# Pads between the tiles: every family of wide fp32r matmuls reads its two operands at another distance modulo 256 bytes

## What is computed

```python
x = x + attn(einsum('bct,bcd->bdt', x, style_w[style]), w_qkv, q_ln, k_ln, w_out)
y = einsum('bsi,boi->bso', x, adapter_w[adapter])
logits = y @ gate_w;  weights = top_k(logits, 2).values
h = relu(y @ up_w) ** 2
shared = h @ down_w
routed = ((y @ fc1_w) @ expert_w * weights.sum(-1)) @ fc2_w
x = x + layernorm(shared + routed) * gamma + beta
```

## Time and the profile before

| | before |
|---|---|
| median of two runs | 1131.38 us |
| the profiled execution's own time | 1133.51 us |
| its span, first to last instruction | 1131.7 us |
| granted TensorE clock, mean | 0.993 of full |
| TensorE matmuls busy | 1095.0 us, 97% |
| TensorE weight loads busy | 891.5 us, 79% |
| GpSimd busy | 714.3 us, 63% |
| VectorE busy | 675.8 us, 60% |
| ScalarE busy | 602.3 us, 53% |
| share of TensorE in the chain that ended last | 95% |

### The profile page before, as it was taken

How to read it: one execution, slowest core, us unless ns; L and a number is a source line. 1 busy time by engine, 2 the same in 40 slices (tenths; PEclk the granted TensorE clock), 3 DMA queues, 4 the chain that set the end, 5 groups by cost and what they waited for, 6 DMA issues and landing times.

```text
span 1131.7 us, 27403 instructions
## 1 busy us (share of the span) xinstructions
PE 1095.0 (97%) x10996; PEld 891.5 (79%) x10996; DVE 675.8 (60%) x1040; ACT 602.3 (53%) x985; POOL 714.3 (63%) x612
## 2 busy tenths in 40 slices
PE   5999999999999999999999999999999999999994
PEld 3877888888888888888877778787878888787883
DVE  5567667666667666766666245565655565554432
ACT  3466767677777677777776425334161625233220
POOL 4565878787878787878676463556455463533332
PEclk9999999999999999999999999999999999999997
DMA  7125464646454646566567953233414123030100
GB/s 275 40 78 167 157 209 159 211 154 212 159 207 158 215 154 213 177 213 157 200 216 253 368 162 90 84 98 104 110 47 135 56 89 98 29 84 28 47 28 37
DMA packets 95292, 160.77 MB, mean 142 GB/s; under 512 B 46400, under 2 KB 47168, under 8 KB 89792
## 3 DMA queue, kind: packets, MB, share of 16 engines
q1 hardware_dynamic: 79456, 118.16, 32.6%
q0 software_dynamic: 12224, 34.10, 9.4%
q10 hardware_dynamic: 3488, 6.78, 1.7%
HBM read 93.97 MB, written 42.47 MB: 121 GB/s over the span
## 4 chain that ended last, share of the span: by engine, by line
PE 95%; DMA 1%; issue 1%; DVE 1%; POOL 0%; ACT 0%; SPq 0%; DVEq 0%; ACTq 0%; POOLq 0%
PE bank L645 24%; PE pair L829 16%; PE bank L805 15%; PE bank L735 10%; PE bank L685 8%; PE bank L822 8%; PE pair L662 3%; PE bank L693 3%; PE pair L707 2%; PE bank L635 2%; PE bank L720 1%; PE bank L775 1%; PE bank L673 1%; DMA xt<-in_x,tile_rows 1%; PE bank L756 0%
## 5 line engine op out<-in xcount | busy, mean ns | idle before, releaser
L1672 POOL TENSOR_TENSOR w_lo<-w2t,w_hi 128x2048 fp32r<-128x2048 f32 x38 | 175.0, 4605 | 35.6 <-ACT w_hi L991 35.5
L645 PE MATMUL bank<-wqkv_hi,h_hi 128*128 128x512 f32 x384 | 154.5, 402 | 0.1
L645 PE MATMUL bank<-wqkv_hi,h_lo 128*128 128x512 f32 x384 | 150.5, 392 | 0.0
L645 PE MATMUL bank<-wqkv_lo,h_hi 128*128 128x512 f32 x384 | 150.3, 391 | 0.0
L1742 POOL TENSOR_TENSOR u_lo<-act,u_hi 128x512 fp32r<-128x512 f32 x64 | 82.8, 1294 | 103.3 <-ACT u_hi L1184 103.2
L829 PE MATMUL pair<-down_hi,u_hi 128*128 128x512 f32 x256 | 101.0, 394 | 0.0
L829 PE MATMUL pair<-down_hi,u_lo 128*128 128x512 f32 x256 | 100.8, 394 | 0.0
L805 PE MATMUL bank<-yT_hi,up_hi 128*128 128x512 f32 x256 | 100.8, 394 | 0.0
L829 PE MATMUL pair<-down_lo,u_hi 128*128 128x512 f32 x256 | 100.3, 392 | 0.0
L805 PE MATMUL bank<-yT_hi,up_lo 128*128 128x512 f32 x256 | 99.8, 390 | 0.0
L1521 DVE TENSOR_TENSOR act<-act 128x512 f32<-128x512 f32 x59 | 67.0, 1136 | 54.6 <-ACT act L1180 54.6
(11 more groups left out here) (178 smaller groups left out, 2910.7 us busy)
## 6 DMA issues: line engine op xcount, KB each, us to landing
w2t<-in_w SPq DMA_DIRECT2D x38, 1024.0 KB
vx<-v_hl SPq DMA_DIRECT2D x128, 68.0 KB
x1g<-x_rows SPq DMA_DIRECT2D x32, 256.0 KB, 3.0
kx<-k_hl SPq DMA_DIRECT2D x124, 64.0 KB
x_rows<-x1t SPq DMA_DIRECT2D x31, 256.0 KB, 3.5
ffn_high<-w_high SPq DMA_DIRECT2D x20, 256.0 KB, 3.5
ffn_low<-w_low SPq DMA_DIRECT2D x20, 256.0 KB, 3.4
stage<-in_wqkv SPq DMA_DIRECT2D x3, 1024.0 KB, 8.1
```

The source lines that it names most:

```text
L645: m = e.matmul(into, a[:, c, :], b[:, n, c, :], start=(c == 0 and k == 0), stop=(c == KC - 1 and k == 2))
L1672: e.tensor_tensor(w2_lo[:, :, :], w2t[:, :, :], w2_hi[:, :, :].bitcast(F32), ALU.subtract).then_inc(d_wlo, 1)
```

## The change

Nothing is computed otherwise and no instruction is added, removed or moved on any engine. Pads are put between tiles, the order of the four `h` tiles is changed, and the four chunks of `gate_hl` are put 256 bytes apart. All tiles behind the first of these edits shift by 768 to 1184 bytes.

```diff
-    gate_hl = sb("gate_hl", [P, KC, 2, EXPERTS], F32R)
+    gate_lines = sb("gate_hl", [P, KC, 64], F32R)
+    gate_hl = gate_lines[:, :, 0:2 * EXPERTS].rearrange("p c (a n) -> p c a n", a=2)
...
     w2_hi = sb("w2_hi", [P, KC, DM], F32R)
+    sb("pad_x", [P, 48])
     xgT_hi = sb("xgT_hi", [P, DM], F32R)
...
-    h_hi = [asb(f"h_hi{i}", [P, KC, P], F32R) for i in range(2)]
-    h_lo = [asb(f"h_lo{i}", [P, KC, P], F32R) for i in range(2)]
+    h_hi, h_lo = [], []
+    for i in range(2):
+        asb(f"pad_h{i}", [P, 8 + 8 * i])
+        h_hi.append(asb(f"h_hi{i}", [P, KC, P], F32R))
+        h_lo.append(asb(f"h_lo{i}", [P, KC, P], F32R))
...
+    asb("pad_kx", [P, 32])
     prep = ExitStack()
...
+    asb("pad_o", [P, 8])
     o_hi = asb("o_hi", [P, BPT, P], F32R)
...
     yt = sb("yt", [P, KC, 2, TOK], U16)
+    sb("pad_y", [P, 24])
     yT_hi = [sb("yT_hi0", [P, KC, TOK], F32R)]
...
-    sb("pad", [P, 160])
+    sb("pad", [P, 192])
     down_hi = sb("down_hi", [P, FC, DM], F32R)
```

## The result

The changed kernel takes **1143.0 us** (median of two runs, 1142.75 to 1143.25) against 1131.38 before. The recorded ratio is 1.0089, with a 95% interval of 1.0067 to 1.011: slower by about 1%, inside the 2% band. The two medians alone give 1.0103, from two runs on each side; why the recorded ratio is lower is not shown. The forecast was 1144.0.

What follows compares the result with a forecast made beforehand. TensorE was taken as the bound, its wide fp32r matmul pace passing into the time one for one. Terms 6.6 - 0.6 + 2.1 + 5.1 - 0.6 = +12.6 us on 1131.38 made 1144.0 us, range 1123 to 1156.

Steps and rivals of the forecast that it cites:

- project: Attention tiles, distance 0 to 32 and 96: 35 steps a tile slower by 6.7 ns, less entry and early waits; +6.0 us.
- adapt_slot: Distance 0 to 192: 10 steps slower by 6.7 ns, less entry, in 38 slots; +2.1 us.
- up: Feed-forward part, distance 0 to 160: 768 steps slower by 6.7 ns; +5.1 us.
- `down`, f = 4: Feed-forward chunk going from distance 128 to 0: 3 x 32 steps faster by 6.7 ns; -0.6 us.
- `out_project`, `down` f = 0 to 3: Distances 64 to 224 and 128 to 160: 233.3 ns before and after; 0, bounds -5.1 to +2.6 us each.
- route products, gates: Feed-forward route products stay at distance 0 and 226.7 ns; gate products go from mixed distances to 224; 0.
- at 226.7 from f = 5 on: Expected sign in the later profile: down x24 falls from 5.56 to 5.54 us, with this step in its later chunks.
- five others at 226.7: Argument that distance matters: two slow families sit at 233, the other families share nothing but their distance.
- Distance is not the cause: Rival: the tiles of down or neighbours of out_project make them slow; nothing moves, 1131.4 us; chance 0.12.
- The starts matter too: Rival: moving operands starting at odd multiples of 32 bytes cost 16 cycles themselves; 1149 us, range 1145 to 1157; chance 0.10.
- Cheap: Rival: new distances step at 220 ns, giving 1103 us, or only one or two do, 1115 to 1130; chance 0.15.
- dearer: Rival: new distances cost two collisions of 16 cycles, 240 ns a step; +34 us, 1165; chance 0.13 for 1152 to 1165.

Runs made afterwards that it cites:

- only_project: Kernel before the change, with project's operands moved to distances 32 and 96 and the other changed families kept at equivalent distances; ratio 1.0058 (1.0046 to 1.0071).
- only_up: Kernel before the change, with up moved to distance 160, down f = 0 to 3 to 32 and gates to 160; ratio 1.0052 (1.0034 to 1.0069).
- all_zero: Kernel before the change, with pads putting every wide matmul family and the gate products at distance 0; median 1126.8 us, ratio 0.9951.
- shift32: Kernel before the change, with one 32-byte pad ahead of gate_raw moving every later tile, all distances kept; ratio 0.9998 (0.9986 to 1.001).

## Why the prediction was right

**The bound.** TensorE's chain passed the slower pace on one for one: from the eighth attention tile to the last its gaps are at most 0.14 us, before and after; where the two parts of the kernel meet, its longest wait is 1.5 us before and 1.4 after. From the start of the ninth tile's `project` to that of the thirty-first, before took 18.88 us a tile and after 19.13: +0.25, where the terms say 0.26. From the first `up` to the last `down`, 511.1 and 516.7 us: +5.6.

**The size for distances that no row showed.** 233.3 ns was taken from 64 and 128 for 32, 96, 160, 192 and 224. Four of five fit within 1 ns; 192 did not. The quantum of 16 cycles is real as a mean at 32, 64, 128, 160 and 224 (558 to 560 cycles), but not as a rule: 192 stands at 549, 96 at 562.

| term | forecast us | measured us, from the pieces |
|---|---|---|
| `project` | +6.0 | +0.20 and +0.22 a tile, less the early tiles: +6.1 (only_project: +6.6) |
| `adapt_slot` | +2.1 | +0.02 in 26 slots, +0.02 to +0.04 in the others: about +0.9 (an estimate; a piece is read to 0.01) |
| `up` | +5.1 | 8 x 0.65 = +5.2 (only_up: +5.9) |
| `down`, f = 4 | -0.6 | 5.56 before and after: 0 |
| `out_project`, `down` f = 0 to 3 | 0 | 0 |
| route products, gates | 0 | 24 x 0.01 - 8 x 0.03 = 0 |
| sum | +12.6 | +12.2; medians +11.6; by the ratio +10.1 (7.6 to 12.4) |

**Two terms were mis-sized, and offset each other in part.** `adapt_slot` was priced at 233.3 and measured 230, because 192 is a cheap distance; 1.3 us too much. For f = 4 I counted three steps at 226.7, but the pace does not follow the distance at once. The distance fell to 0 at the 13th matmul in place of the 16th, and yet the steps from the 13th to the 21st take 1.85 us in both kernels and only the last three are at 226.7: the three matmuls that were won went into a longer settling, eight steps in place of five (974.88 - 973.73 = 1.15 us, 230 ns each, in the earlier trace rows). That is 0.6 us too much gain, and "at 226.7 from f = 5 on" was wrong for the same reason.

**A reading that was off.** The prediction set "five others at 226.7" against two slow families. There are four (`project`, `adapt_slot`, `up`, route products) and the end of `down`; `gate_products` stood at 233.8, and all_zero shows that the distance does not change that.

**The rivals.** "Distance is not the cause" fell with all_zero and shift32: the step of a matmul of 512 columns is 16 cycles longer or not through nothing but the distance between its two kinds of operands. The Trainium skill, "SBUF — State Buffer", section "Who interferes with whom", gives TensorE two independent read ports and says that it never waits on anyone. The runs here do not agree, for these shapes: `down` x24 went from 5.56 to 5.44 us by a move of its tiles. Whether the ports themselves or something behind them is where it waits, no run shows. "The starts matter too" fell with shift32. "Cheap" got one of its five distances, "dearer" none. The size was no more than well placed between them: that 32, 96, 160 and 224 would stand near 64 and 128 was taken over from two samples, and 192, 240 and 248 show that it need not have held.

**The start-up.** The second tile's `project` begins at 34.30 us before and at 31.64 after, in the chains. This isn't the change: shift32, which steps like before, has 31.80, all_zero 34.17. Two things make up the 2.7 us. The gathered x that TensorE's first `style` waits for came later: that `style` begins at 25.17 us before and at 23.99 after, 1.2 us. And TensorE's granted clock: from 27 to 29 us it is 0.50 before (the 1.2 GHz level) and 1.00 after. In front of the drop TensorE had waited 3.0 us for that x, after the change 2.0. So the x24 of the first `project` took 7.08 us before and 5.60 after, 1.5 us. all_zero has the same low stretch (0.50 from 26 to 28 us, behind a wait of 2.8), shift32 has none (1.00, a wait of 2.1): in these four traces the low clock goes with the longer wait, not with the pads. This start-up is why the two spans are nearer than the medians.

## What to carry to other kernels

Where TensorE is the bound and wide fp32r matmuls follow each other with a new stationary operand each, put the moving and the stationary tiles at the same address modulo 256 bytes. It costs a pad of under 256 bytes and was worth 3% of each such matmul, 0.5% of this kernel; a shift of all starts by 32 bytes was free. To find it, compare the step from start to start between families of one shape: a difference of a few nanoseconds with everything else equal is a finding. And when a family gets to distance 0 from another distance, or from behind small matmuls, do not count on the cheap pace at once. The settling took from none to ten steps in the `project` tiles of the kernel before, five steps in its `down`, eight in `down` after, at some 230 to 232 ns, and none in `down` of only_up; what sets its length stays open.

## What the runs showed that I had not expected

- The curve is no window: 240 (16 bytes behind) at 227.7 ns and 192 at 228.9 are nearly as cheap as 0, while 248, between 240 and 0, is at 233.3. Which resource has that pattern stays open.
- The cost is in the step of the matmuls alone; the weight loads of the wide families with 128 columns last 187 to 189 ns at every distance of the runs.
- At a fixed dear distance the steps are not alike: they alternate between 238 and 229 ns at 128 in `down` and between 236 and 231 at 64 in `out_project`, and go round in threes (232, 238, 231) at 160 in `down`, with means within a nanosecond of each other.
- With 16 stationary columns distance 0 brings nothing: 8 gate products took 1.86 us at 0 and 1.84 at 224.
- No wide matmul family settled below 226.7 ns, 544 cycles for 512 columns. Whether the 32 cycles beyond are a fixed cost or a part of the same conflict was not tried: no version here runs wide matmuls without a weight load beside them.
